# Last stage of a vision tokenizer with a state scan and routed experts: variance and one-hot rows by TensorE, B/C/z scaled into SBUF, new places of parts, loads on two queues

## The reference

```
t = unfold3(t, stride 2);  h = t @ proj_w.T + proj_b                 # 768 channels
x = layernorm(h)
B = x @ W_B + b_B;  C = x @ W_C + b_C
delta = softplus(x @ W_D + b_D + p_Delta)                            # z = x @ W_D
a = exp(delta * A);  b = (a - A) / (delta * A) * delta * B
s = a * s + b * x  (over tokens, 16 states a channel);  h += sum_n C_n s_n
x = layernorm(h)
e = x @ enc_w + enc_b;  p = softmax(e @ sw_w + sw_b)
onehot = one_hot(argmax(p))
out = h + (gelu(x @ w1_e + b1_e) * onehot @ w2 + onehot @ b2) * max(p)
```

## Time and profile before

| | us |
|---|---|
| median of 3 executions | 8267.98 (8265.39 to 8268.63) |
| the profiled execution | 8263.06, span 8261.3 |
| TensorE busy | 7327.8 (89%) |
| VectorE busy | 6205.4 (75%) |
| GpSimd busy | 5547.7 (67%) |
| ScalarE busy | 4337.3 (53%) |
| last stage, from its first load to the end | 3108.9 to 8261.3 |
| its first scan | 3222.7 |

### The profile page before, as it was taken

One profiled execution on the slowest core, in us unless ns is written; L12 is line 12 of the kernel. 1 busy time (PEld: TensorE's weight loads), 2 busy tenths in 40 slices (PEclk: granted clock), 3 DMA queues, 4 the chain that ended last, 5 costly groups with the idle time before them and its releaser, 6 DMA issues.

```text
span 8261.3 us, 86870 instructions
## 1 busy us (share of the span) xinstructions
PE 7327.8 (89%) x31004; PEld 2931.6 (35%) x31004; DVE 6205.4 (75%) x6573; ACT 4337.3 (53%) x7781; POOL 5547.7 (67%) x2487
## 2 busy tenths in 40 slices
PE   8999999869999975688888888888888888888987
PEld 6444444324444421133333333333333333333323
DVE  2566666742333345999999999999999999999995
ACT  3666666753444433555555555555555555555552
POOL 0111111148766614989999889999889998889994
PEclk9999999989999987789999889998989998988988
DMA  1111111135554413233333333333333333333331
GB/s 40 34 47 42 46 43 38 45 77 114 102 103 100 102 34 107 93 124 120 120 110 116 114 124 120 120 110 116 111 128 120 120 110 116 110 126 122 121 107 54
DMA packets 358648, 786.32 MB, mean 95 GB/s; under 512 B 72229, under 2 KB 284726, under 8 KB 350728
## 3 DMA queue, kind: packets, MB, share of 16 engines
q1 hardware_dynamic: 322168, 690.47, 28.4%
q0 software_dynamic: 21712, 51.75, 2.5%
q10 hardware_dynamic: 14336, 38.54, 1.3%
HBM read 597.06 MB, written 183.35 MB: 94 GB/s over the span
## 4 chain that ended last, share of the span: by engine, by line
DVE 28%; PE 15%; issue 11%; POOL 4%; ACT 4%; DMA 0%; DVEq 0%; SPq 0%; ACTq 0%; POOLq 0%
DVE v L2038 13%; DVE v L2047 13%; PE ps L1665 3%; POOL v L1634 3%; PE ps L1670 2%; PE ps L1672 2%; PE ps L1734 2%; PE ps L1679 2%; POOL v L1622 1%; DVE dl L2028 1%; PE ps L1681 1%; PE ps L1785 1%; ACT ps L1928 1%; ACT gm L1952 1%; PE ps L1798 0%
## 5 line engine op out<-in xcount | busy, mean ns | idle before, releaser
L2047 DVE TENSOR_TENSOR_SCAN v<-ps,v 128x901 f32<-128x901 f32 x1344 | 2732.1, 2033 | 95.0 <-DVE v L2038 2.7
L1634 POOL TENSOR_TENSOR v<-v,ct 128x1792 f32<-128x1792 f32 x672 | 2257.6, 3360 | 479.0 <-ACT st L1889 477.8
L1622 POOL TENSOR_TENSOR v<-xr,bt 128x1792 f32<-128x1792 f32 x672 | 2258.1, 3360 | 82.3 <-DMA xr<-h_by_channel 82.3
L1928 ACT ACTIVATE ps<-dr,aa 128x448 f32<-128x448 f32 x2688 | 1595.9, 626 | 1319.6 <-DVE v L2047 1303.2
L2038 DVE SCALAR_TENSOR_TENSOR v<-ps,aa,v 128x448 f32<-128x448 f32 x2688 | 1687.5, 669 | 71.5 <-ACT ps L1928 67.9
L1734 PE MATMUL ps<-v,dg 128*32 128x448 f32 x5376 | 792.3, 632 | 616.2 <-POOL v L1634 395.1
L236 POOL DMA_DIRECT2D tokens<-ob x448 | 235.3, 532 | 1529.9 <-DVE ob L563 1486.9
L1798 PE MATMUL ps<-w_or_w,gm 128*112 128x384 f32 x1792 | 694.4, 535 | 3.0 <-DMA w_or_w<-in_w 3.0
L1665 PE MATMUL ps<-h,w_or_w 128*128 128x448 f32 x1344 | 588.7, 592 | 84.9 <-DVE bcs L2022 84.9
L1889 ACT ACTIVATE st<-v 128x4 f32<-128x4 f32 x672 | 140.9, 210 | 893.5 <-DVE v L2047 893.5
L1670 PE MATMUL ps<-x,wpa 128*128 128x448 f32 x1008 | 497.1, 632 | 7.6 <-DVE w_or_w L2154 6.9
(11 more groups left out here) (328 smaller groups left out, 11558.6 us busy)
## 6 DMA issues: line engine op xcount, KB each, us to landing
xr<-h_by_channel SPq DMA_DIRECT2D x168, 896.0 KB, 4.9
dr<-delta_by_channel SPq DMA_DIRECT2D x168, 896.0 KB, 4.7
x<-tokens SPq DMA_DIRECT2D x252, 224.0 KB, 5.3
tokens<-ob POOLq DMA_DIRECT2D x448, 112.0 KB, 2.4
w_or_w<-in_w SPq DMA_DIRECT2D x29, 1536.0 KB, 6.4
w_or_w<-centred_w SPq DMA_DIRECT2D x27, 1536.0 KB, 9.0
h_by_channel<-h SPq DMA_DIRECT2D x112, 336.0 KB, 4.8
delta_by_channel<-dl SPq DMA_DIRECT2D x224, 168.0 KB, 2.8
```

Of the source, the lines that this page charges most:

```text
L1622: tt(v[:, n % RING, :, 2:T + 2], xr[:, dc % 2, :].rearrange("p (i t) -> p i t", i=4), bt[:, q:q + 1, :].to_broadcast([128, 4, T]), ALU.mul ...
L1634: tt(v[:, n % RING, :, 2:T + 2], v[:, n % RING, :, 2:T + 2], ct[:, q:q + 1, :].to_broadcast([128, 4, T]), ALU.mult).then_inc(s_cm, 1)
L1928: fn(decay(g), dr[:, dc % 2, g, :], ACT.Exp, scale=aa[:, 4 * k + g:4 * k + g + 1]).then_inc(s_a, 1)
L2047: nc.vector.tensor_tensor_scan(row, flat[:, 1024 * pair + 1:1024 * pair + GW + T + 2], row, 0.0, ALU.mult, ALU.add).then_inc(s_sc, 1)
```

## The change

- B, C and z: the first operation writes the scaled rows into `bcs` (SBUF) and no longer back into PSUM. The bias is then added in `bcs` itself, rows of C and z first, and the rows of B are biased and scaled from `bcs`. The banks are free at the first of the three (`s_bn` instead of `s_bcs`).
- Second variance: ScalarE writes the square of the mean and a copy of the mean of squares into `rs2`, and the product that spreads the row subtracts them (a -1 in `pick`). VectorE's subtraction is gone.
- One-hot rows: TensorE adds the token means to the turned rows in PSUM with one more product, and ScalarE copies the result. VectorE's addition is gone.
- New places in the tables for most of these parts.
- Beginning: the loads alternate between SP's and ScalarE's queue; the load of w1 comes after the first x; `front(0)` is issued ahead of the product and the subtraction for w1; the store of the centred w1 moves into step 1 of unit 0; x is spread before B, C and delta, and three of the four C spreads come after the first delta.

```diff
--- before.py
+++ after.py
@@ -1447,15 +1446,15 @@
         s_oa = sem("t_out_written")
         s_out = [sem("t_out_stored_even"), sem("t_out_stored_odd")]
 
-        P_PJ, P_SUM, P_Z = (1, 3, 4, 5, 7, 8), (9, 11), 14
-        A_HW, A_SQ, A_MU, A_RS = (5, 6.5, 8, 9, 10.5, 12), (9.5, 12.5), 15, 14.5
-        A_MX, A_SP = (17, 17.5), ((18, 18.5), (19, 19.5))
+        P_PJ, P_SUM, P_Z = (1, 3, 4, 5, 7, 8), (9, 11), 15
+        A_HW, A_SQ, A_MU, A_RS = (4, 6.5, 8, 9.5, 10.5, 12), (9.5, 12.5), 15.5, 15.5
+        A_MX, A_SP = (17.5, 17.5), ((18, 18.5), (19, 19.5))
         V_BC, V_DL = 15, (18, 19)
-        P_SUM2, P_VAR, P_IN, P_LOG, P_TURN = (2, 4), 6, (10, 12, 13, 14), 8, 11
-        P_MASK, P_OUT = (15, 15, 17, 17), (18, 19, 20, 20, 21, 22, 23, 24)
-        A_SQ2, A_MS, A_RS2, A_EX, A_GL = (1, 5.5), 8, 9.5, 12, 17
+        P_SUM2, P_VAR, P_IN, P_LOG, P_TURN = (2, 4), 6, (10, 11, 13, 14), 8, 10
+        P_MASK, P_OUT = (15, 15, 16, 17), (18, 19, 20, 20, 21, 22, 23, 24)
+        A_SQ2, A_MS, A_RS2, A_EX, A_OH, A_GL = (1, 5.5), 7.5, 9.5, 12, 14, 17
         A_OUT = (22, 22.5, 23.5, 24, 25, 26, 27, 28)
-        V_VAR, V_ENC, V_IN, V_LOG, V_EQ, V_OH, V_MASK = 7, 9, (12, 14, 15, 16), 11, 12, 13, (17, 17, 18, 18)
+        V_ENC, V_IN, V_LOG, V_EQ, V_MASK = 9, (12, 14, 16, 16), 10, 11, (17, 17, 19, 19)
         ROUTE, TAIL = 9, 29
 
         def means(i):
@@ -1552,24 +1551,23 @@
                             sp.wait_ge(s_cv if own else s_cm, 2 * owned(n) if own else others(n))
                     spread_row(ct[:, q, :], i, 1, q).then_inc(s_lc[q], 16)
 
-            for dst, src in loads:
+            for dst, src in loads[0::2]:
                 sp.dma_start(dst, src).then_inc(s_w, 16)
-            sp.dma_start(w1, w["w1"]).then_inc(s_wv, 16)
             sp.wait_ge(s_set, 9)
             load_x(0)
-            sp.wait_ge(s_pd, 16)
-            sp.dma_start(w1c, w1).then_inc(s_w1c, 16)
-            sp.wait_ge(s_w1c, 16)
+            sp.dma_start(w1, w["w1"]).then_inc(s_wv, 16)
+            store_h(0)
+            spread_x(0, 0)
             load_x(1)
-            store_h(0)
             store_bc(0)
             for q in range(Q):
                 spread_b(0, q)
-                spread_c(0, q)
-            spread_x(0, 0)
+            spread_c(0, 0)
             store_delta(0, 0)
             spread_delta(0, 0)
             store_delta(0, 1)
+            for q in range(1, Q):
+                spread_c(0, q)
             for i in range(UNITS):
                 for k in range(STEPS):
                     if k % 4 == 0 and k < STEPS - 4:
@@ -1579,7 +1577,11 @@
                         spread_b(i, 3)
                     if i >= 1 and k < 3:
                         spread_c(i, k + 1)
+                    if k == 1 and i == 0:
+                        sp.wait_ge(s_pd, 16)
+                        sp.dma_start(w1c, w1).then_inc(s_w1c, 16)
                     if k == 4 and i >= 2:
+                        sp.wait_ge(s_w1c, 16)
                         sp.wait_ge(s_o, 2 * NCH * (i - 1))
                         sp.dma_start(w1, w1c).then_inc(s_wv, 16)
                     if k == 13 and i + 2 < UNITS:
@@ -1700,7 +1702,7 @@
                         after(pe, s_dl, DC * i)
                     if dc == 1:
                         after(pe, s_oa, 2 * NCH * (i - 2))
-                        after(pe, s_bcs, 2 * i)
+                        after(pe, s_bn, i)
                     if dc >= 2:
                         pe.wait_ge(s_hw, DC * i + (dc - 1 if dc < 4 else 4))
                     if dc == 5:
@@ -1715,7 +1717,7 @@
                 if k == P_SUM[1]:
                     sums_1(i, range(3, DC))
                 if k == P_Z:
-                    pe.wait_ge(s_bcs, 2 * (i + 1))
+                    pe.wait_ge(s_bcs, 2 * i + 1)
                     pe.wait_ge(s_hw, DC * (i + 1))
                     after(pe, s_he, MT * (i - 2) + 2)
                     mm(bank(BF), pick[mid, 0, :], bcs[mid, :], start=True, stop=True).then_inc(s_z, 1)
@@ -1744,9 +1746,9 @@
                 if k == P_SUM2[1]:
                     sums_2(i, range(3, DC))
                 if k == P_VAR:
-                    pe.wait_ge(s_vr, i + 1)
+                    pe.wait_ge(s_ms, 2 * (i + 1))
                     pe.wait_ge(s_hw, min(DC * (i + 2) + 3, DC * UNITS))
-                    mm(bank(BF), pick[mid, 1, :], rs2[mid, :], start=True, stop=True).then_inc(s_vs, 1)
+                    mm(bank(BF), pick[:, 1, :], rs2[0:64, :], start=True, stop=True).then_inc(s_vs, 1)
                 for m in range(MT):
                     if P_IN[m] != k:
                         continue
@@ -1759,7 +1761,7 @@
                     if m == 2:
                         pe.wait_ge(s_oh, i + 1)
                     if m == 3:
-                        pe.wait_ge(s_bcs, 2 * min(i + 3, UNITS))
+                        pe.wait_ge(s_bn, min(i + 3, UNITS))
                         pe.wait_ge(s_mu, min(i + 3, UNITS))
                     over_chunks(bank(in_bank(m)), lambda dc: w1[:, dc, 128 * m:128 * m + 128], i).then_inc(s_hm, 1)
                 if k == P_LOG:
@@ -1769,9 +1771,11 @@
                     last.then_inc(s_lgp, 1)
                 if k == P_TURN:
                     pe.wait_ge(s_r, ROUTE * (i + 1))
+                    pe.wait_ge(s_mu, i + 1)
+                    mm(ps[few, BX, 0:T], ident[few, few], means(i), start=True, stop=False)
                     for ch in range(NCH):
-                        last = mm(ps[few, BX, ch * CH:ch * CH + CH], eq[:, ch, :], ident[0:CH, 0:CH],
-                                  start=True, stop=True)
+                        last = mm(ps[few, BX, ch * CH:ch * CH + CH], eq[:, ch, :], ident[0:CH, 0:CH], start=False,
+                                  stop=(ch == NCH - 1))
                     last.then_inc(s_tr, 1)
                 for m in range(MT):
                     if P_MASK[m] != k:
@@ -1809,14 +1813,17 @@
             for dc in range(DC):
                 last = mm(bank(BX, NR), jm[:, :], enc[:, dc, :], start=(dc == 0), stop=(dc == DC - 1))
             last.then_inc(s_pm, 1)
+            pe.wait_ge(s_pd, 14)
+            for k in range(STEPS):
+                front(0, k)
             pe.wait_ge(s_wv, 16)
+            pe.wait_ge(s_bn, 1)
+            pe.wait_ge(s_mu, 1)
             for dc in range(DC):
                 last = mm(bank(BS, NX * NR), jm[:, :], w1[:, dc, :], start=(dc == 0), stop=(dc == DC - 1))
             last.then_inc(s_pm, 1)
             pe.wait_ge(s_dgm, 1)
             pe.wait_ge(s_pd, 16)
-            for k in range(STEPS):
-                front(0, k)
             for i in range(UNITS + 1):
                 for k in range(TAIL if i == UNITS else STEPS):
                     if i < UNITS:
@@ -1937,7 +1944,8 @@
                     squares(i, 1, range(3, DC))
                 if k == A_MS:
                     act.wait_ge(s_var[1], DC * (i + 1))
-                    fn(rs2[mid, :], ps[low, BX, 0:T], ACT.Square).then_inc(s_ms, 1)
+                    fn(rs2[low, :], ps[low, BX, 0:T], ACT.Square).then_inc(s_ms, 1)
+                    fn(rs2[mid, :], ps[mid, BX, 0:T], ACT.Copy).then_inc(s_ms, 1)
                 if k == A_RS2:
                     act.wait_ge(s_vs, i + 1)
                     fn(rs2[:, :], bank(BF), ACT.Ln, bias=eps[:, :]).then_inc(s_ln[1], 1)
@@ -1946,6 +1954,10 @@
                 if k == A_EX:
                     act.wait_ge(s_r, ROUTE * i + 3)
                     fn(ex[:, :, :], lg, ACT.Exp).then_inc(s_rx, 1)
+                if k == A_OH:
+                    act.wait_ge(s_tr, i + 1)
+                    after(act, s_o, 2 * NCH * i)
+                    fn(oh8, ps[few, BX, 0:T], ACT.Copy).then_inc(s_oh, 1)
                 if k == A_GL:
                     for m in range(MT):
                         act.wait_ge(s_he, MT * i + m + 1)
@@ -1974,8 +1986,10 @@
                     front(i + 1, k)
 
             act.sem_inc(s_in, 1)
+            for dst, src in loads[1::2]:
+                act.dma_start(dst, src).then_inc(s_w, 16)
             act.wait_ge(s_w, 16 * len(loads))
-            act.wait_ge(s_pd, 16)
+            act.wait_ge(s_pd, 14)
             act.wait_ge(s_set, 9)
             act.preload_act_table_set(BOTH)
             for k in range(2 * STEPS):
@@ -2015,11 +2029,10 @@
                     dve.wait_ge(s_rs[0], i + 1)
                     after(dve, s_bst, 32 * i)
                     after(dve, s_z, i)
-                    rows = ps[0:49, BS, 0:T]
-                    tt(rows, rows, rs1[0:49, :], ALU.mult).then_inc(s_bn, 1)
+                    tt(bcs[0:49, :], ps[0:49, BS, 0:T], rs1[0:49, :], ALU.mult).then_inc(s_bn, 1)
                     dve.wait_ge(s_bn, i + 1)
-                    stt(bcs[br, :], ps[br, BS, 0:T], bbc[br, :], rs1[br, :], ALU.add, ALU.mult).then_inc(s_bcs, 1)
-                    ts(bcs[zr, :], ps[zr, BS, 0:T], bbc[zr, :], None, ALU.add).then_inc(s_bcs, 1)
+                    ts(bcs[zr, :], bcs[zr, :], bbc[zr, :], None, ALU.add).then_inc(s_bcs, 1)
```

(11 more changed lines are left out.)

## The result

The changed kernel takes 8212.2 us (median of 4, 8207.9 to 8220.9) against 8267.0 of the kernel before, a ratio of 0.9934 (95% interval 0.9918 to 0.9950): 55 us faster. The forecast was 8286. The measured time lies inside the range, but on the other side of no change than the forecast case.

The account below looks back on a forecast made before the run. VectorE was taken to bound the kernel. Terms of -5.6 - 1.65 + 5.9 + 1.4 + 1.1 = +1.15 us a unit over 26 units, with first and last units, beginning and end, gave +18: 8286 us, range 8120 to 8340.

Parts of the forecast that it names:

- the forecast case: Whole kernel: both SBUF-only operations of B, C and z held by GpSimd, 8286 us, chance 0.62.
- What bounds the kernel: Last stage, unit of 24 steps: VectorE bounds, working 167.4 of 177 us, the rest being its waits.
- Work taken from VectorE: Variance subtraction and one-hot copy leave VectorE: -1.65 us a unit.
- The old waits: VectorE's waits for mask products, expert products and decays lose their cause through new places: -5.6 us a unit.
- The hold: At B, C and z, GpSimd's running instructions hold VectorE's tensor_scalar and scalar_tensor_tensor: +5.9 us a unit.
- Rivals 1 and 2: At B, C and z: only the tensor_scalar is held, 8185, chance 0.15; nothing is held, 8097, chance 0.12.
- +1.4 for expert product 0: TensorE waits for chunk 3 before projection 4, so expert product 0 ends after VectorE arrives: +1.4 us a unit.
- +1.1 for z and the decays of step 18: Masks at the lower clock with z behind them make Relu and decays of step 18 late: +1.1 us a unit.
- Beginning: Before the first scan: loads on two queues 3.5, w1 product later 3.4, delta store earlier 5: -12 us.
- an edge of its own, 8225: The forecast case without the new waits at product 0 and z: 8225 us.
- the dear edge: The forecast case with all bounds on the dear side: 8340 us.
- The other rivals: TensorE stays at 1.2 GHz through projection 5, 8415, chance 0.06; places don't take effect, 8370 or 8205, 0.05 together.

Follow-up runs that it names:

- e10: e1 with both the variance subtraction (step 7) and the one-hot addition (step 12) back on VectorE: 8118.9 us.
- e11: e1 with the variance subtraction alone back on VectorE: 8086.6 us.
- e1: The changed kernel with B, C and z scaled in PSUM and biased from there again, tensor_scalar still first: 8054.0 us.
- e7: The changed kernel with GpSimd's two multiplications beside B, C and z cut from 448 to 16 columns: 8057.3 us.
- e12: e1 with only the rows of C and z scaled into SBUF and biased there, B from PSUM, one more scaling: 8146.1 us.
- e5: e1 with the routing comparison put back to step 12, behind the first expert scaling: 8083.3 us.
- e13: The changed kernel with the products of masks 0 and 1 issued twice each: 8285.7 us.
- e4: The kernel before with the new beginning alone: 8254.0 us.
- e3: The kernel before with the new tables of places alone: 8142.6 us.
- e6: e1 with chunk 3 copied out of its bank at step 9 instead of 9.5: 8054.4 us.
- e9: e1 with the routing comparison back at step 12 and chunk 3 copied at step 9: 8081.6 us.

## Why the prediction was wrong, step by step

- **What bounds the kernel**: right. VectorE's work and waits alone make up the difference between scans to 1.1 us.
- **Work taken from VectorE** (-1.65 a unit): right in size for the changed kernel, whose account closes with it to 1.1 us. As e10 and e11 show, putting the operations back costs more than this, since the chain behind them then makes VectorE wait.
- **The old waits** (-5.6): right. 155.9 us fall to 4.0, 152 less; the sum took away 5.6 x 26 + 2.4 = 148.
- **The hold** (+5.9): right in its mechanism and its size. 27 operations of each kind grew by 155.5 us, 5.8 a unit; e1, e7 and e12 show who holds and for how long. Rivals 1 and 2 fall. The Trainium skill (SBUF — State Buffer, Who interferes with whom) gave the same lock for a whole instruction: the trace and e7 agree with it, but for one hold over three of GpSimd's instructions (below).
- **The step that failed first: +1.4 for expert product 0.** Its first half held: TensorE did wait for chunk 3, 2.92 us where 3.1 was forecast. The lines of the changed kernel:

```profile
5373.89 4.17 PE L1672 MATMUL ps<-x,wpa 128*128 128x448 f32 x6 [2.92 <-ACT h L1859]
...
5394.59 4.78 PE L1667 MATMUL ps<-h,w_or_w 128*128 128x448 f32 x12
...
5397.27 2.03 DVE L2060 TENSOR_TENSOR_SCAN v<-ps,v 128x901 f32<-128x901 f32 x1
5399.40 0.62 DVE L2100 TENSOR_TENSOR gm<-ps,rs2t 128x448 f32<-128x448 f32 x1
```

  And VectorE's last scan ahead of product 0 in the kernel before:

```profile
5417.07 2.03 DVE L2047 TENSOR_TENSOR_SCAN v<-ps,v 128x901 f32<-128x901 f32 x1
```

  The two sides of the wait were sized wrong. Both are counted here from the moment at which TensorE starts projection 4, forecast at 5393.9. The product was forecast 1.4 behind VectorE, which comes to it at 5419.1 in the trace of before and 0.8 earlier without the variance: 5418.3 + 1.4 - 5393.9 = 25.8 us for the product, 24.4 for VectorE. In the changed kernel the product ends 5399.37 - 5373.89 = 25.5 us behind that start, as the lower clock cost 1.6 and not 2.0 (4.17 for six matmuls instead of 2.56). VectorE comes 5399.30 - 5373.89 = 25.4 us behind it, 1.0 later than forecast: the prediction says itself that the routing comparison moves ahead of `V_IN[0]`, but leaves its six small operations out of VectorE's arrival. So 1.4 - 1.0 - 0.3 leaves 0.1, and the trace has no margin either way: in 11 of the 26 units `V_IN[0]` starts without a wait, in 14 it starts 0.03 to 0.20 us behind its scan, and once 1.39. e5 shows the forgotten term: with the comparison behind `V_IN[0]`, the wait is 1.06 us a unit.
- **The step that failed second: +1.1 for z and the decays of step 18.** The prediction let TensorE do masks 0 and 1 in 3.35 us at the lower clock and z behind them; z's two passes at that clock are 1.7 us more, by the four of the masks. In the trace of the changed kernel they lie side by side:

```profile
5434.94 1.11 PE L1789 MATMUL ps<-wpb 9*128 9x448 f32 x1 [6.07 <-DVE gm L2100]
5435.58 1.08 PE L1723 MATMUL ps<-bcs,pick 32*128 32x448 f32 x1
5435.85 0.95 PE L1789 MATMUL ps<-wpb 9*128 9x448 f32 x1
5436.46 0.95 PE L1723 MATMUL ps<-bcs,pick 32*128 32x448 f32 x1
5436.60 1.69 PE L1789 MATMUL ps<-wpb 9*128 9x448 f32 x2
```

  Six passes take 3.35 us, exactly what the four of the masks took by themselves before, at the same granted clock of 0.50, the lower level of 1.2 GHz (window, length, busy, granted clock, DMA share, GB/s):

```profile
5434.90:5436.90 2.00, 1.96 (x5) 0.50 0.97 404
```

  The inputs of z lie in rows 32 to 63 and those of the masks in rows 64 to 72; the masks, all on the same rows, still follow one another. The Trainium skill (TensorE: Matmul & The Clock Gate, Part 3: Packing small matmuls — row/col tiling) says that small products placed in different groups of 32 rows of the array run at the same time. The trace agrees, and the prediction didn't use it; no run moves z onto the rows of the masks, so that the rows decide is not shown by an experiment. All of it is over at 5438.29, and ScalarE comes to the Relu at 5438.78, behind the decays of step 17; with 1.7 us more it would have been 1.2 late. The decays of step 18 end at 5443.22 and VectorE takes them at 5443.32, 0.1 later: 1.2 less 0.1 is the forecast's 1.1. e13 shows that a delay here counts nearly in full.
- **Beginning** (-12): right in its sum, -12.7 by the traces and -13 by the medians of e4. In the two profiled kernels only 8.1 of it shows at the first scan, since the stage of the changed kernel started 4.4 us later (3113.34 against 3108.90). In the profiles of the thirteen experiments this start lies between 3108.6 and 3115.2, with the old beginning as with the new, so the 4.4 says nothing of the change.
- **Sum.** Without the two terms, 2.5 x 26 = 65 us, the sum of the prediction is -47 instead of +18: 8216 for the profiled execution against 8211.4 measured. That it closes so well is luck in part: the waits fell 4 us further than forecast, and the late start of the stage took 4 back. The prediction had named this case as an edge of its own, 8225; by its terms this edge is 8286 - 65 = 8221, and the dear edge is 8286 + 26 x (0.3 + 0.3 + 0.9) + 4 = 8329, not 8340.
- **The other rivals.** TensorE's clock did not stay low: it was 0.62 from 5373 to 5376, 0.81 to 5379 and 1.00 to 5382. The places did take effect (e3).

## What to carry to other kernels

A tensor_scalar from SBUF to SBUF and a scalar_tensor_tensor with two SBUF inputs cost here what was left of GpSimd's running instruction, 3.4 and 3.7 us for work of 0.44 and 0.67; reading PSUM for the same sum was worth 158 us. So look at the inputs of every small operation beside a busy GpSimd, and at its kind. Not every operation in SBUF alone is held. The routing comparison of the changed kernel has two, a tensor_reduce and a reciprocal, and they never took more than 0.18 us (min/median/max in ns):

```profile
L2112 DVE TENSOR_REDUCE sm<-ex x28: 173/176/180, 3463.5 to 8140.6; 112x4 f32<-112x32 f32 x28
L2115 DVE RECIPROCAL sm<-sm x28: 166/166/169, 3463.9 to 8140.9; 112x4 f32<-112x4 f32 x28
```

In one unit they start at 5391.81 and 5392.12, while GpSimd's instructions run from 5388.86 to 5392.24 and from 5392.18 to 5395.56. They have 32 and 4 columns; no run has them at 448.

When a new wait is forecast as a difference of two arrivals, both have to be worked out again with everything that was moved: 1 us forgotten on one side decides. And before products are added up on TensorE, look at which rows their inputs lie in: here two passes of z added nothing to four of the masks.

## What was not expected of the hardware

In the first unit of the loop the tensor_scalar took 8.20 us. It was issued at 3318.53, while GpSimd worked through three instructions without a gap:

```profile
3316.48 3.36 POOL L1624 TENSOR_TENSOR v<-xr,bt 128x1792 f32<-128x1792 f32 x1
3319.80 3.35 POOL L1636 TENSOR_TENSOR v<-v,ct 128x1792 f32<-128x1792 f32 x1
3323.12 3.36 POOL L1624 TENSOR_TENSOR v<-xr,bt 128x1792 f32<-128x1792 f32 x1
...
3318.53 8.20 DVE L2034 TENSOR_SCALAR bcs<-bcs,small 17x448 f32<-17x448 f32 x1
```

It ended at 3326.73, 0.25 us after the third. At step 15 of the later units it got its turn between two instructions that follow one another as closely (5423.87 to 5424.11), and GpSimd's next one lasted 3.51 instead of 3.36. So the end of GpSimd's instruction doesn't always hand over; what decides was not tried.

Taking TensorE's wait for chunk 3 away did not raise its clock as a whole: in e6 the slow six matmuls are those of projection 5 (4.25 us) instead of projection 4. The lower clock came behind TensorE's next waits instead (0.45 and 0.71 us ahead of projection 5), and cost the same. But e9 has these two waits as well (0.44 and 0.71), and there the six matmuls of projection 5 took 2.67 us (mean of all matmuls of this line from 3480 to 7900: 573 ns, 605 in e6). What decides between the two is open.
